# FFN pieces in new slots, and the last operation of each Runge-Kutta stage in two halves

## The reference, cut to what matters

```
def _derivative(q, p, drive, coupling, bias):
    dq = q - q**3/3 - p + drive + tanh(q) @ coupling.T + bias
    dp = EPSILON * (q + ALPHA - BETA*p)
def _rk4_step(q, p, drive, coupling, bias):      # DT = 0.01
    k1 at (q, p); k2 at q + DT/2*dq1; k3 at q + DT/2*dq2; k4 at q + DT*dq3
    q_next = clip(q + DT/6*(dq1 + 2*dq2 + 2*dq3 + dq4), -20, 20)     # p_next likewise
```

## Time and profile before

| | us |
|---|---|
| median of 3 runs (lowest, highest) | 1643.82 (1642.74, 1644.45) |
| the profiled execution, its own time | 1640.76 |
| its span, first to last instruction | 1638.8 |
| TensorE busy, matmuls | 1489.4 |
| VectorE busy | 1119.8 |
| ScalarE busy | 588.7 |
| GpSimd busy | 381.5 |

### The profile page before, as it was taken

The page is one execution under the profiler, slowest core; times in us unless marked ns, Lnnn a source line. Parts: engine busy times, 40 slices in busy tenths (PEclk is TensorE's granted clock), DMA queues, the critical chain, the costliest instruction groups (busy, mean ns, idle before and its releaser), DMA issues.

```text
span 1638.8 us, 46339 instructions
## 1 busy us (share of the span) xinstructions
PE 1489.4 (91%) x16583; PEld 927.8 (57%) x16624; DVE 1119.8 (68%) x3565; ACT 588.7 (36%) x1903; POOL 381.5 (23%) x545
## 2 busy tenths in 40 slices
PE   5999999996799999999999997678899999999984
PEld 1333333334575767667675844556666666666662
DVE  1667667765774747575664732578888888888886
ACT  1444444441102020201102021455555555555552
POOL 0221221210000000000000000245655555556550
PEclk8999999997899999999999998999999999999996
DMA  7111112116101000100000024001111111111111
GB/s 304 44 45 50 51 46 65 51 47 167 9 1 26 0 26 0 26 0 26 6 19 13 13 64 163 21 25 29 40 40 40 33 35 32 35 32 43 37 38 33
DMA packets 91035, 72.79 MB, mean 44 GB/s; under 512 B 32480, under 2 KB 82912, under 8 KB 89824
## 3 DMA queue, kind: packets, MB, share of 16 engines
q1 hardware_dynamic: 71184, 59.35, 12.4%
q10 hardware_dynamic: 18032, 6.88, 1.7%
q0 software_dynamic: 1760, 5.77, 1.2%
HBM read 55.03 MB, written 16.94 MB: 44 GB/s over the span
## 4 chain that ended last, share of the span: by engine, by line
PE 73%; DVE 13%; ACT 5%; issue 5%; DMA 1%; POOL 1%; DVEq 0%; SPq 0%; POOLq 0%; ACTq 0%
PE ps L655 13%; PE ps L645 13%; PE ps L750 11%; PE ps L583 11%; PE ps L595 10%; PE ps L689 3%; PE ps L713 3%; ACT mem L961 3%; DVE mem L1313 2%; DVE mem L1271 2%; PE ps L740 2%; ACT ps L953 2%; PE ps L764 1%; PE ps L666 1%; DVE ps L1281 1%
## 5 line engine op out<-in xcount | busy, mean ns | idle before, releaser
L750 PE MATMUL ps<-mem 128*32 128x128 f32 x8192 | 278.8, 276 | 68.5 <-ACT mem L961 65.8
L750 PEld LDWEIGHTS ps<-mem 128*32 128x32 f32 x8192 | 211.4, 110 | 143.0 <-ACT mem L961 97.2
L645 PE MATMUL ps<-mem 128*128 128x512 f32 x512 | 224.6, 592 | 0.0
L655 PE MATMUL ps<-mem 128*128 128x256 f32 x1024 | 222.3, 379 | 0.0
L655 PEld LDWEIGHTS ps<-mem 128*128 128x128 f32 x1024 | 194.0, 190 | 26.0
L509 POOL TENSOR_TENSOR mem<-mem 128x128 f32<-128x128 f32 x64 | 30.8, 481 | 732.8 <-ACT mem L956 732.8
L583 PE MATMUL ps<-mem 128*32 128x384 f32 x2048 | 181.6, 497 | 10.2 <-DMA mem<-in_W_ih 6.3
L595 PE MATMUL ps<-mem 128*32 128x384 f32 x2048 | 177.6, 488 | 2.4 <-DVE mem L1098 2.4
L928 ACT ACTIVATE mem<-mem 128x512 f32<-128x512 f32 x32 | 19.7, 630 | 391.0 <-DVE mem L1211 391.0
L645 PEld LDWEIGHTS ps<-mem 128*128 128x128 f32 x512 | 95.6, 190 | 109.7 <-issue 109.3
L961 ACT ACTIVATE mem<-mem 128x64 f32<-128x64 f32 x512 | 102.9, 248 | 116.5 <-DVE mem L1271 116.4
(11 more groups left out here) (139 smaller groups left out, 2097.0 us busy)
## 6 DMA issues: line engine op xcount, KB each, us to landing
mem<-x_scr SPq DMA_DIRECT2D x128, 64.0 KB, 1.8
mem<-in_xT SPq DMA_DIRECT2D x64, 64.0 KB, 1.9
mem<-in_Wq SPq DMA_DIRECT2D x1, 4096.0 KB, 12.4
mem<-in_Wo SPq DMA_DIRECT2D x1, 4096.0 KB, 20.7
mem<-in_x SPq DMA_DIRECT2D x16, 256.0 KB, 2.8
x_scr<-mem SPq DMA_DIRECT2D x32, 128.0 KB, 2.3
q_scr<-mem SPq DMA_DIRECT2D x64, 64.0 KB, 1.6
mem<-q_scr SPq DMA_DIRECT2D x64, 64.0 KB, 1.9
```

What stands on the lines that cost most here:

```text
L645: mm = pe.matmul(ps[:, 6 + pr, :], aoT[:, h, pr * P:pr * P + P], wo[:, h, :], start=(h == 0), stop=(h == HEADS - 1))
L655: mm = pe.matmul(ps[:, h % Q_BANKS, 0:BLK], wq[:, c, h * DH:(h + 1) * DH], xnb[:, c, :], start=(c == 0), stop=(c == NC - 1))
L750: mm = pe.matmul(ps[32 * j:32 * j + 32, st % 2, 0:P], thT[:, c, :], ct[:, c, j * P:(j + 1) * P], start=False, stop=(c == NC - 1), skip_gro ...
```

## The change

The FFN's pieces are put in other slots, and some products are split over two slots. The parts of t are now 640 and 768 columns. In each stage the final operation is done as two operations of 64 columns, with the first half's transpose between them. The next step's seed goes between the two transposes of a fourth stage. On ScalarE the square goes between the two tanhs. On VectorE the pieces of a slot go ahead of the cube and of the seed of the next stage. On SyncE the stores of output and the x1 loads go behind the tile's loads. The core of the diff:

```diff
-GU_SLOTS = (11, 12, 13, 15, 0, 1, 3, 4)
-DOWN_SLOTS = (5, 7, 8, 9)
-T_PARTS = ((0, 6 * P), (6 * P, INNER))
+GU_SLOTS = {11: ((0, 0, NC), (1, 0, 2)), 12: ((1, 2, NC), (2, 0, 2)), 13: ((2, 2, NC),), 15: ((3, 0, NC),),
+            0: ((4, 0, NC), (5, 0, 1)), 1: ((5, 1, NC),), 3: ((6, 0, NC),), 4: ((7, 0, NC),)}
+DOWN_SLOTS = {5: (0, 2), 7: (2, 7), 8: (7, 10), 9: (10, IC)}
+T_PARTS = ((0, 5 * P), (5 * P, INNER))
...
@@ SyncE, group
-                    if s == 2 and out_tile is not None:
-                        tile_store(out_tile)
-                    if s == 2 and x1_tile is not None:
-                        tile_x1(x1_tile)
                 if g is not None:
                     tile_loads(g)
+                if out_tile is not None:
+                    tile_store(out_tile)
+                if x1_tile is not None:
+                    tile_x1(x1_tile)
...
@@ GpSimd, slot
-                    if k in (13, 14):
-                        gate_scaled(i, k - 13)
+                    if k in (13, 15):
+                        gate_scaled(i, k // 15)
...
-                    if k in (12, 15) and rk:
-                        t_rounded(i, k // 15)
+                    if k in (11, 14) and rk:
+                        t_rounded(i, k // 14)
...
-                if i is not None and k == 11 and rk:
+                if i is not None and k == 15 and rk:
                     pool.wait_ge(f_ysc, i + 1)
...
@@ TensorE
+            def products(i, k):
+                for order, lo, hi in GU_SLOTS.get(k, ()):
+                    product(i, order, lo, hi)
+
+            def down(lo, hi):
+                for c in range(lo, hi):
                     mm = pe.matmul(ps[:, 7, :], t8T[:, c, :], wdT[:, c, :], start=(c == 0), stop=(c == IC - 1))
...
@@ ScalarE, stage
-                if st:
-                    squared()
                 for half in range(2):
                     act.wait_ge(rk_qT, 2 * n + half + 1)
                     act.activation(thT[:, 2 * half:2 * half + 2, :], qsT[:, 2 * half:2 * half + 2, :], ACT.Tanh).then_inc(rk_th, 1)
+                    if st and half == 0:
+                        squared()
...
@@ ScalarE, slot
-                    if k in (13, 14):
-                        silu_part(i, k - 13)
+                    if k in (13, 15):
+                        silu_part(i, k // 15)
...
@@ VectorE, stage
+                fill()
                 dve.wait_ge(rk_sq, n + 1)
                 stt(out=ebuf, in0=ps[:, 5, 0:P], scalar=KEPT[st], in1=qs, op0=ALU.subtract, op1=ALU.mult).then_inc(rk_e, 1)
                 if st < 3:
                     seed(t, s, st + 1)
-                fill()
...
                 dve.wait_ge(rk_e, n + 1)
                 dve.wait_ge(rk_mm, n + 1)
                 dst = qst[st] if st < 3 else ps[:, 4, 2 * P:3 * P]
-                stt(out=dst, in0=ps[:, st % 2, 0:P], scalar=STEP[st], in1=ebuf, op0=ALU.mult,
+                low, high = slice(0, P // 2), slice(P // 2, P)
+                stt(out=dst[:, low], in0=ps[:, st % 2, low], scalar=STEP[st], in1=ebuf[:, low], op0=ALU.mult,
+                    op1=ALU.subtract).then_inc(rk_low, 1)
+                dve.wait_ge(rk_low, n + 1)
+                if not (end and st == 3):
+                    turned_half(dst, 0)
+                stt(out=dst[:, high], in0=ps[:, st % 2, high], scalar=STEP[st], in1=ebuf[:, high], op0=ALU.mult,
                     op1=ALU.subtract).then_inc(rk_qs if st < 3 else rk_pre, 1)
                 if st < 3:
                     dve.wait_ge(rk_qs, n + 1)
+                    turned_half(dst, 1)
                 else:
-                    dve.wait_ge(rk_pre, t + 1)
-                if not (end and st == 3):
-                    state_turned(dst)
-                if st == 3:
                     if not end:
                         seed(t + 1, (s + 1) % 4, 0)
+                    dve.wait_ge(rk_pre, t + 1)
+                    if not end:
+                        turned_half(dst, 1)
...
@@ VectorE, slot: gate_part 1 from slot 13 to 14, ahead of gated_part 0
@@ t_added 0 from 11 to 10, t_grid 1 from 10 to 11, t_added 1 from 15 to 13, the scaled output from 10 to 15
```

More of the change, by code:

```diff
@@ L754, in stage, with product @@
                     mix_into(t, s, st + 1)
[L756 to L763, removed]
+            def product(i, order, lo, hi):
+                kind, m = GU_ORDER[order]
+                gate = kind == "g"
+                if lo == 0:
+                    wait_if(pe, *{0: (f_gated, GU_T * i - 1), 1: (f_gated, GU_T * i), 2: (f_gsc, GU_T * i + 1), 3: (f_gsc, GU_T * i + 2),
+                                  4: (f_gated, GU_T * i + 1), 5: (f_gsc, GU_T * i + 3), 6: (f_gated, GU_T * i + 2),
+                                  7: (f_gsc, GU_T * i + 4)}[order])
+                for c in range(lo, hi):
                     mm = pe.matmul(ps[:, 2 + order % 2, 0:GU_N], qxT[:, c, :], (wgT if gate else wuT)[:, c, m * GU_N:(m + 1) * GU_N],
                                    start=(c == 0), stop=(c == NC - 1))
-                mm.then_inc(f_g if gate else f_u, 1)
+                if hi == NC:
+                    mm.then_inc(f_g if gate else f_u, 1)
             def t_turned(i, half):
@@ L788, in slot @@
                         pe.wait_ge(f_qTcp, i + 1)
-                    if k in GU_SLOTS[:4]:
-                        product(i, *GU_ORDER[GU_SLOTS.index(k)])
+                    if k >= 11:
+                        products(i, k)
                 i = tile(1)
                 if i is not None:
-                    if k in GU_SLOTS[4:]:
-                        product(i, *GU_ORDER[GU_SLOTS.index(k)])
+                    if k < 11:
+                        products(i, k)
                     if k == 15:
@@ L803, in slot @@
                         pe.wait_ge(f_tTcp, 2 * i + 1)
-                    if k == 8:
+                    if k == 7:
                         pe.wait_ge(f_tTcp, 2 * i + 2)
                     if k in DOWN_SLOTS:
-                        down(i, DOWN_SLOTS.index(k))
-            def down(i, part):
-                for c in range(3 * part, min(3 * part + 3, IC)):
+                        down(*DOWN_SLOTS[k])
+            def products(i, k):
+                for order, lo, hi in GU_SLOTS.get(k, ()):
+                    product(i, order, lo, hi)
+            def down(lo, hi):
+                for c in range(lo, hi):
                     mm = pe.matmul(ps[:, 7, :], t8T[:, c, :], wdT[:, c, :], start=(c == 0), stop=(c == IC - 1))
-                if part == 3:
+                if hi == IC:
                     mm.then_inc(f_y, 1)
@@ L1266, in _, with turned_half @@
             dve.wait_ge(rk_bits, 1)
+            def turned_half(src, half):
+                dve.transpose(qsT[:, 2 * half:2 * half + 2, :].rearrange("p c b -> p (c b)"), src[:, half * 64:half * 64 + 64]).then_inc(rk_qT, 1)
             def state_turned(src):
-                for half in range(2):
-                    dve.transpose(qsT[:, 2 * half:2 * half + 2, :].rearrange("p c b -> p (c b)"), src[:, half * 64:half * 64 + 64]).then_inc(rk_qT, 1)
+                turned_half(src, 0)
+                turned_half(src, 1)
             state_turned(qn[3])
@@ L1306, in stage @@
                     seed(t, s, st + 1)
-                fill()
-                if st == 0 and not (last and s == 3):
+                if st == 0 and not end:
                     drive_sum(t + 1, (s + 1) % 4, g + 1 + (s == 3))
@@ L1353, in slot @@
                         v.did(dve.tensor_copy(xsx, xnew))
-                    if k in (12, 13):
-                        if k == 12:
-                            v.need(v.n)
-                        gate_part(i, k - 12)
+                    if k == 12:
+                        v.need(v.n)
+                        gate_part(i, 0)
                     if k == 14:
+                        gate_part(i, 1)
                         gated_part(i, 0)
@@ L1380, in slot @@
                     if k == 10:
+                        t_added(v, 0)
+                    if k == 11:
                         t_grid(v, 1)
-                    if k == 11:
-                        t_added(v, 0)
-                    if k == (15 if rk else 11):
+                    if k == (13 if rk else 11):
                         t_added(v, 1)
@@ L1389, in slot @@
                 i = tile(2)
-                if i is not None and k == 10:
+                if i is not None and k == (15 if rk else 10):
                     v.need(v.n)
```

2 lines of the change are left out of this document (1 added, 1 removed).

## The result

The changed kernel took 1647.51 us (median of 11 runs, 1644.69 to 1648.84), the kernel before 1641.14 beside it (11 runs, 1636.68 to 1644.45). The ratio is 1.0037, with a 95% interval of 1.0026 to 1.0048: slower by more than the 0.2% bound, where I had forecast slower, at 1651.6 against 1643.8. Forecast was +0.5%, measured +0.37%.

The account below looks back on a forecast made before the run. TensorE was 73% of the chain, but neither it nor VectorE was simply full; VectorE's order set first stages. Fourteen groups' +8.4 us, less 0.4 each in groups 0 and 1, plus 0.2 tail gave +7.8: 1643.8 to 1651.6, range 1636 to 1661.

Parts of the forecast that it names:

- The late seed: Second and third stages: pieces ahead delay seed, then mixing, product and next piece; these stages lose 1.55 us a group.
- The halves: Final operation in two: 0.22 us per half, first tanh at 0.53, weights at 0.84, a chain-only stage 2.06.
- the sum: Stage-by-stage addition over a settled group: 36.87 us against 36.27, and +7.8 us for the whole kernel.
- The locks: VectorE and GpSimd lock each other out in stages 8 (2.72 us) and 14 (2.39); without them 2.21 and 2.26.
- TensorE 0.97 + 1.08 + 0.14 = 2.19 decides: Stages 0, 4, 12: weights' start, TensorE's work and the gap to the final operation set 2.19 us, before 2.53.
- fourteen groups carry nearly all pieces ... groups 0 and 1 win 0.4 each: Scaling to sixteen groups: fourteen together lose 8.4 us, while groups 0 and 1, with few pieces, win 0.4 each.
- The tail: The 46 us after the last stage: the last down projection waits for its second part, +0.2 us.
- Cover holds: Rival, chance 0.2: pieces' inputs are ready when VectorE asks and GpSimd lets go; a group 35.7, time 1635 us.
- The seed's wait is dear: Rival, chance 0.1: mixing starts 0.12 behind the seed and reductions hold VectorE 0.51; a group 37.6, time 1662 us.
- The case of no change: Rival, chance 0.2: cheaper halves and a shorter chain of waits; a group 36.5 or 36.3, time 1641 to 1647 us.
- GpSimd's clamp: Could hold the first stage's seed: 0.02 in stage 8, 0.3 in stage 0 if GpSimd's rounding runs late; +4 us.
- nothing is wanted sooner: SyncE's queue: nothing besides the moved stores and loads is wanted sooner than 6.9 us between last store and slot 3.

Follow-up runs that it names:

- the experiment: Changed kernel with the final operation whole again, seed behind both transposes and square ahead of the tanhs, pieces still ahead: 1640.66 us, ratio 0.9984, a group 36.33.
- the run at 1710: Changed kernel with SyncE's output stores and x1 loads put back in slot 11: 1710.16 us, ratio 1.0404 against the kernel before.

## Why the forecast held, and where its sum was off

**The late seed.** Right in place and size. Slot 1 was 2.39 for 2.38, slot 2 2.66 for 2.68, slot 6 2.44 for 2.44; the mixing starts at 2.53 of slot 1 for 2.52, 0.06 behind the seed's end. Shown by three kernels: the move of the pieces alone costs 0.84 in the old slots and 0.58 in the new, and taking it back outside the first stages brings slots 2, 5, 6, 10 and 13 to 2.13.

**The halves.** 0.22 for the first half, 0.18 to 0.20 for the second (0.22 taken); first tanh at 0.53 to 0.55 (0.53), weights at 0.84 (0.84), a free stage 2.07 (2.06). That they win where the chain over ScalarE and TensorE is last, and lose where VectorE is, was in the sum. What they cost was in it only through single stages; the whole, 0.63, came from the experiment. It holds for halves, square and seed together.

**The locks.** Slot 8 2.68 for 2.72, slot 14 2.34 for 2.39. The second lock is there as well: in slot 13 VectorE's long add ends at 1.73 and GpSimd's add (L510) at 2.05, 0.32 behind (0.31 taken), and the piece of slot 14 starts at 1.44 (1.49). I priced the lock at 0.51 in slot 8. The mask's extra length is measured, 1.00 for 0.48; what the stage would be without the lock is not, since moving the mask out (2.64 to 2.25, without halves) takes the mask's own work out too, and shortening the add made it worse. One thing in the earlier trace rows I had the wrong way round: GpSimd was not late but early there, its second operation 1.48 into the stage against 1.94 in a settled group, and so ahead of the mask at 1.90.

**First stages.** The term "TensorE 0.97 + 1.08 + 0.14 = 2.19 decides" held in slots 4 and 12 (2.19, 2.20). In slot 0 it failed, 2.38: I took the seed-to-clip spacing of 0.17 also for clip to piece, and where the loop jumps back that is 0.38, hidden before behind the wait for the square. Piece, cube, seed and drive sum are then VectorE's, and VectorE decides. This is +0.19 in eleven groups.

**Small misses.** Slots 3 and 15 are 0.06 and 0.11 over: their weights wait for TensorE, which the six mixings of the stage ahead hold about 0.1 longer than I had taken. Slot 5 is 0.09 under. The settled group came out 0.09 over the forecast.

**Why the total was less.** A group was forecast at +0.60 and measured at +0.70, but the total was forecast at +7.8 and is +6.8 in the span (+6.4 between the medians). The step that failed is "fourteen groups carry nearly all pieces ... groups 0 and 1 win 0.4 each": groups 0, 1, 2 and 15 won 3.5 together where the sum had -0.8 for two and +1.2 for the other two. Groups 0 and 1 won 0.95 and 0.43; with few pieces in them nearly every stage is 0.06 shorter by the halves. Groups 2 and 15 won 1.18 and 0.89, and not for want of late products: their slots 1 and 2 are 2.38 and 2.66 to 2.67, as in a settled group. Before the change these two groups were not settled ones of 36.27 but took 37.50 and 37.70, mostly because slot 8 was 3.29, with the mask held by GpSimd's second operation. That is the earlier trace rows, which the sum had in hand and did not use here. After the change slot 8 is 2.48 and 2.57 in them. The tail was +0.8, not +0.2; what in it I have not tested. And 1.4 of the +6.8 lies ahead of the scan, where nothing was changed. That the total came within 1.0 us of the forecast is therefore in part luck: groups 2 and 15 (3.3 under the sum) hide a settled group that was longer than forecast (1.1 over in eleven groups), the tail and those 1.4.

**The rivals.** "Cover holds" needed product 4 by 0.85 of slot 1; it came at 1.06. "The seed's wait is dear" fell by the 0.06. The case of no change needed 0.20 for a half and a seed seen at once; the half was 0.22 and the seed 0.06. GpSimd's clamp held no seed in the settled groups: the next seed starts 0.55 into slots 0 and 8.

**SyncE.** The sum had nothing for its move, and no loss by it is seen in the changed kernel. The ground given, that nothing is wanted sooner, missed what the move is for, as the run at 1710 showed.

## What to carry to other kernels

In this kernel an operation that starts another engine's queue (the seed of 0.28 us) belongs ahead of work that may wait, and what may go ahead of it had to be decided stage by stage: only the first stage of a step has the slack. Splitting an operation in halves shortens the path through the next engines by 0.06 us and makes the engine that issues it 0.2 later for its next work, 0.35 where that work first waits for the square; it paid only in stages where that engine was not the later one. When two engines lock each other out, look at which starts first and at what stands next in the other's queue: 0.04 us ahead or 0.12 behind made the difference between 0.48 and 1.50 us, and shortening the blocker let the next one in.

## What the runs showed of the hardware that I had not expected

- At the eleven jumps back of the loop (into groups 4 to 14) the VectorE operation behind the clip starts 0.38 to 0.42 us after the clip's start, in the changed kernel and in the one with halves in fourth stages; into groups 2, 3 and 15, where nothing jumps back, and in slots 4, 8 and 12 of every group from 2 on, it is 0.18. The trace shows where it goes: after the loop's branch (L104) VectorE's sequencer records nothing for 0.24 to 0.27 us at these eleven jumps, and 0.05 at the twelfth, which isn't taken; then come two register instructions, and 0.05 behind the second the piece starts (1304.68 and 1304.73 in slot 0 above). No run changes the loop by itself. With a whole final operation the distance is 0.33 to 0.39, and costs nothing there.
- A VectorE mask that GpSimd holds ends 0.34 to 0.35 us after GpSimd's operation does, in three kernels with starts 0.12, 0.25 and 0.62 behind GpSimd's: 1.50, 1.39 and 1.00 us for 640 columns, where 640 columns alone take 0.45 to 0.49. For 768 columns it is 0.41 to 0.42 (0.82 and 1.27 us, alone 0.52 to 0.56).
- Of the two 64-column halves, with a transpose between them, the first takes 0.21 to 0.23 us and the second 0.18 to 0.20 (0.22 in a few), and one of 128 columns takes 0.28 to 0.30: halving the columns leaves two thirds to three quarters of the time.
